# Writing the padding records in the placing stage, instead of filling whole regions during the first attention stage

## The chip, the cores and the metric

The kernel runs on one core of a Trainium2 chip. The metric is the device time of one execution in microseconds (us), as the median of several runs. The engines are TensorE (PE, with its weight loads PEld), VectorE (DVE), ScalarE (ACT), GpSimd (POOL) and SyncE (SP), which here only issues transfers (DMAs) from its own queue.

## The reference

Two transformer-like layers over 4 x 1024 tokens of 128 channels. Each of four blocks is followed by a residual addition and a layer norm:

```
x = ln(x + attention0(x))      # 8 heads, softmax
x = ln(x + ffn0(x))            # small attention, then 8 experts, top 2, gelu
x = ln(x + attention1(x))      # projections, a convolution, a scan
x = ln(x + ffn1(x))            # 8 experts, of which the last chosen one counts
```

What matters here is the last block. Its router chooses the two best of 8 experts for each token, and for expert `i` in order of number `out = where(weight_i > 0, y_i, out)`. So only the chosen expert with the higher number leaves its result, and the kernel computes one expert for each token:

```
wi = w_flat[:, i:i + 1]
h = relu(einsum('nd,hd->nh', x_flat * wi, w1[i]) + b1[i])
y = einsum('nh,dh->nd', h, w2[i]) + b2[i]
out = where(wi > 0, y, out)
```

## The kernel before

The program is a chain of stages. Each is a block in which the five engines run their own programs and meet at semaphores. A block ends with a barrier that waits for all engines. Three stages bear on the change.

`first_attention_stage` (L226) goes through 32 heads of 128 tokens, in loops of four. TensorE projects keys and queries, makes scores and mixes values; VectorE takes maxima, ScalarE exponentials, and GpSimd scales values. SyncE copies each head's keys to the other half of the partitions (`double`, L287), one head ahead. TensorE waits for this (`keys_doubled`) before a head's scores. Between these, SyncE issues one item for each head from a list: 13 loads of constants and then the filling. The filling writes blank records to `scratch`, a table in device memory in which each of the 8 experts has a region of `REGION` = 4096 + 128 rows of 136 floats. `rows_of(e)` (L294) loads the output rows of the blank records of expert `e` into the tile `blank`, and `fill(e)` (L301) writes the whole region from it in two transfers. For `e` = 8 it writes the last 8 tiles behind the regions. GpSimd clears `blank` first (L461). VectorE's first two instructions of the stage are memsets (L439, L440), for which TensorE waits.

`place_stage` (L1893) is the first part of the last block. TensorE turns the 32 tiles of 128 tokens and computes router logits, in 4 batches of 8 tiles. For each batch VectorE chooses the expert, scales the records, weighs them and computes each token's row in `scratch` (`choose`, `scale`, `weigh`, `put`). GpSimd then scatters the batch's 8 tiles to those rows, one indirect transfer of 128 rows each (L2189). After the last batch `start` holds the first free row behind each expert's records. `table` (L2145) works out from it the list of up to 40 tiles that hold records, as `tile_expert` and `tile_base`. The last tile of an expert is partly blank, and tiles behind the last one used are blank wholly; these rows go to output rows behind the end. SyncE's program is short:

```
sp.wait_ge(table_made, 1)
first = [sp.value_load(tile_base[0:1, t:t + 1], ...) for t in range(PER)]   # PER = 4
sp.wait_ge(scattered, 16 * TILES)
for t in range(PER):
    sp.dma_start(sorted_records[:, t, :], scratch[ds(first[t], TILE), :]) ...
```

`sorted_experts_stage` (L2194) loads the other 36 tiles of `scratch` by their addresses (L2252), one `value_load` and one transfer of 68 KB each, and runs each tile through its expert.

Of the kernel before, what the change touches and what calls it, by code (L numbers as in the profile page):

```python
# [7 lines left out]
F32 = mybir.dt.float32  # L8
# [4 lines left out]
ds = bass.ds  # L13


D = 128
B, S = 4, 1024
N = B * S
TILE = 128
# [6 lines left out]
E = 8  # L26


SORT_TILES = (N + E * (TILE - 1)) // TILE + 1
SORT_TILES += -SORT_TILES % 4  # L30
TABLE = SORT_TILES + 2
REGION = N + TILE
UNUSED = 8
RECORD = D + 8
DUMP = E + UNUSED
BLANK_ROWS = 8
U32 = mybir.dt.uint32
I32 = mybir.dt.int32
# [187 lines left out]
def first_attention_stage(core, xT, y, w_q, w_k, values, loads, scratch, blank_rows):  # L226

# [10 lines left out]
    with ExitStack() as st:  # L238
# [28 lines left out]
        blank = core.sb("a_blank", [D, BLANK_ROWS, RECORD], F32, st)  # L267
        blank_zero = core.sem("a_blank_zero")
        blank_rows_in = core.sem("a_blank_rows_in")
        filled = core.sem("a_filled")  # L270
# [11 lines left out]
        with nc.Block() as block:  # L282

            @block.sync
            def _(sp):
# [8 lines left out]
                def rows_of(e):  # L294

                    sp.wait_ge(blank_zero, 1)
                    if e:
                        sp.wait_ge(filled, 32 * e)
                    sp.dma_start(blank[:, :, D:].bitcast(U32), blank_rows[:, e, :, :]).then_inc(blank_rows_in, 16)

                def fill(e):  # L301

                    sp.wait_ge(blank_rows_in, 16 * (e + 1))
                    all_rows = blank[:, :, :].rearrange("p j d -> p (j d)")
                    at = e * REGION
                    if e == E:
                        at += (SORT_TILES - UNUSED) * TILE
                        sp.dma_start(scratch[at:at + UNUSED * TILE, :].rearrange("(p j) d -> p (j d)", j=BLANK_ROWS),
                                     all_rows).then_inc(filled, 16)
                        return  # L310
                    wide = [D, N // (D * BLANK_ROWS), BLANK_ROWS * RECORD]
                    sp.dma_start(scratch[at:at + N, :].rearrange("(c p j) d -> p c (j d)", p=D, j=BLANK_ROWS),
                                 all_rows.unsqueeze(1).broadcast_to(wide)).then_inc(filled, 16)
                    sp.dma_start(scratch[at + N:at + REGION, :].rearrange("(p j) d -> p (j d)", j=BLANK_ROWS),
                                 all_rows[0:TILE // BLANK_ROWS, :]).then_inc(filled, 16)

                double(0, 0)
                for head in range(TILES):
                    double(head + 1, (head + 1) % 2)
                    if head < len(loads):  # L320
                        to, at = loads[head]
                        sp.dma_start(to, at).then_inc(loaded, 16)
                    else:
                        e, at = divmod(head - len(loads), 2)
                        if e <= E:
                            if at == 0:
                                rows_of(e)
                            else:
                                fill(e)
                sp.wait_ge(filled, 16 * (2 * E + 1))  # L330
# [129 lines left out]
            def _(pool):  # L460
                nc.gpsimd.memset(blank[:, :, :], 0.0).then_inc(blank_zero, 1)  # L461
# [1425 lines left out]

PER = BANK // D

def place_stage(core, src, mean_w, ident, router, order, records, scratch, tile_expert, tile_base, loads, sorted_records,  # L1893
# [18 lines left out]
    tile_rows, rows_of_out = order[:, at:at + TABLE], order[:, at + TABLE:at + TABLE + TILES]  # L1912
    at += TABLE + TILES
    region, earlier_first = order[:, at:at + E], order[:, at + E:at + 2 * E]
    with ExitStack() as st:
# [5 lines left out]
        eps = core.sb("p_eps", [D, 1], F32, st)  # L1921
        turned = core.ps("p_turned", [TILE, 2, BANKS, BANK], st)
# [39 lines left out]
        recorded = core.sem("p_recorded")  # L1962
# [701 lines left out]
```

## Time and profile before

| | |
|---|---|
| median of 3 runs | 1737.61 us (1737.19 to 1740.08) |
| the profiled execution's own time | 1737.19 us |
| its span in the trace | 1735.3 us |
| TensorE busy | 1545.1 us, 89% |
| VectorE, ScalarE, GpSimd busy | 1321.8, 1288.9, 542.7 us |
| placing stage | about 1564.7 to 1630.4 us of the span |

The time is that of the execution on the device; the span runs from the first to the last instruction that the profiler recorded, 1.9 us shorter. Busy times count no register, semaphore or DMA-issuing instructions. All times below are counted from the start of the span.

### The profile page before, as it was taken

The page shows a single profiled execution, that of the slowest core. Times are in us where ns is not written, and L with a number is a line of the kernel's source. Part 1 is how long each engine was busy: PE and PEld are TensorE (multiplying, and loading weights), DVE is VectorE, ACT ScalarE, POOL GpSimd, SP SyncE. Part 2 cuts the span into 40 slices and gives each one's busy share as a digit, 9 for nine tenths or more (in the row PEclk, how much of TensorE's full clock was granted, in tenths as well). Part 3 has the DMA queues.
Part 4 walks back from the last instruction along what each step waited for, and adds up shares of the span by engine and source line. Part 5 has one row for each costly group of instructions (what it writes and reads, how often), then busy time and mean ns, then how long its engine had stood idle before and what let it go on. Part 6 is the DMA issues. An engine that isn't in the chain of part 4 may idle for free. (4 is left out here: it accounts for less than half of the span.)

```text
span 1735.3 us, 38769 instructions
## 1 busy us (share of the span) xinstructions
PE 1545.1 (89%) x13958; PEld 839.0 (48%) x13958; DVE 1321.8 (76%) x1885; ACT 1288.9 (74%) x2465; POOL 542.7 (31%) x757
## 2 busy tenths in 40 slices
PE   5999999999988999999999999998899965664397
PEld 4555555555553344343434444346677721223286
DVE  2777777777759999999999999954655447985475
ACT  2777777777763899989988989986688758753187
POOL 0222222222236110101011011205799805543466
PEclk8999999999995999999999999998999976886599
DMA  2121123232204010011001100005254300003220
GB/s 75 29 87 59 54 73 111 86 125 73 85 19 123 21 31 15 5 21 31 7 5 31 32 5 26 17 3 101 49 99 90 58 16 0 1 0 139 57 66 32
DMA packets 49388, 84.83 MB, mean 49 GB/s; under 512 B 19232, under 2 KB 25128, under 8 KB 48752
## 3 DMA queue, kind: packets, MB, share of 16 engines
q1 hardware_dynamic: 43888, 76.25, 16.9%
q0 software_dynamic: 5376, 6.96, 1.5%
q8 instruction: 73, 1.20, 0.3%
q14 instruction: 51, 0.42, 0.1%
HBM read 32.78 MB, written 23.92 MB: 33 GB/s over the span
## 5 line engine op out<-in xcount | busy, mean ns | idle before, releaser
L1050 ACT ACTIVATE m_probs<-m_ring 128x512 f32<-128x512 f32 x1024 | 543.1, 598 | 76.2 <-PE m_ring L966 60.4
L1129 DVE TENSOR_REDUCE m_half_max<-m_pairs 128x2 f32<-128x1024 f32 x512 | 587.9, 1215 | 11.1 <-PE m_pairs L949 10.6
L436 DVE TENSOR_REDUCE a_neg_max<-a_scores 128x1 f32<-128x1024 f32 x257 | 310.5, 1215 | 90.7 <-PE a_scores L363 90.7
L424 ACT ACTIVATE a_probs<-a_scores,a_neg_max 128x1024 f32<-128x1024 f32 x256 | 285.4, 1115 | 123.4 <-DVE a_neg_max L436 123.4
L981 PE MATMUL m_acc<-m_probs,m_v_aug 128*32 128x256 f32 (+1 forms) x4032 | 325.9, 396 | 0.0
L966 PE MATMUL m_ring<-m_q_max,m_k 32*128 32x512 f32 x1024 | 317.9, 497 | 4.0 <-DVE m_q_max L1143 2.9
L949 PE MATMUL m_pairs<-m_k,m_q 32*128 32x512 f32 x1024 | 263.4, 512 | 13.0 <-DVE m_half_max L1129 9.6
L363 PE MATMUL a_scores<-a_q,a_k_own 64*128 64x512 f32 x516 | 259.9, 620 | 6.5 <-ACT a_probs L424 5.6
L363 PE MATMUL a_scores<-a_q,a_k_other 64*128 64x512 f32 x516 | 258.3, 620 | 0.8 <-ACT a_probs L424 0.3
L966 PEld LDWEIGHTS m_ring<-m_q_max,m_k 32*128 32x128 f32 x1024 | 146.7, 183 | 216.9 <-ACT m_probs L1050 109.5
L472 POOL TENSOR_TENSOR a_scaled<-values,a_inv 128x128 f32<-128x128 f32 x256 | 102.0, 399 | 365.7 <-DVE a_inv L454 234.8
L1495 POOL TENSOR_TENSOR e_g_parts<-e_gated,e_g_parts 128x512 fp32r<-128x512 f32 x128 | 165.6, 1326 | 37.8 <-ACT e_g_parts L1420 36.4
L1454 DVE TENSOR_TENSOR e_gated<-e_up,e_gates 128x512 f32<-128x512 f32 x128 | 87.2, 690 | 86.8 <-ACT e_up L1413 78.7
L373 PE MATMUL a_mixed<-a_probs,a_scaled 128*32 128x128 f32 x4128 | 139.2, 276 | 0.0
L981 PEld LDWEIGHTS m_acc<-m_probs,m_v_aug 128*32 128x32 f32 x4032 | 79.8, 108 | 122.7 <-ACT m_probs L1050 70.6
L373 PEld LDWEIGHTS a_mixed<-a_probs,a_scaled 128*32 128x32 f32 x4128 | 104.9, 109 | 56.2 <-issue 30.3
L363 PEld LDWEIGHTS a_scores<-a_q,a_k_other 64*128 64x128 f32 x516 | 86.0, 187 | 65.4 <-issue 32.7
L949 PEld LDWEIGHTS m_pairs<-m_k,m_q 32*128 32x128 f32 x1024 | 97.3, 187 | 28.0 <-DVE m_half_max L1129 23.1
L1413 ACT ACTIVATE e_up<-e_up,e_b 128x512 f32<-128x512 f32 x128 | 84.4, 660 | 32.7 <-PE e_up L1370 32.6
L363 PEld LDWEIGHTS a_scores<-a_q,a_k_own 64*128 64x128 f32 x516 | 86.0, 187 | 33.2 <-issue 24.3
L1229 POOL CAST m_max_cols<-m_row_max 128x16 fp32r<-128x16 f32 x32 | 6.8, 212 | 281.8 <-DVE m_row_max L1135 281.1
L1420 ACT ACTIVATE e_g_parts<-e_gated 128x512 fp32r<-128x512 f32 x128 | 79.7, 624 | 7.8 <-DVE e_gated L1454 7.8
(283 smaller groups left out, 2151.7 us busy)
## 6 DMA issues: line engine op xcount, KB each, us to landing
sorted_tokens<-a_blank SPq DMA_DIRECT2D x8, 2176.0 KB
e_gates<-sorted_results SPq DMA_DIRECT2D x64, 256.0 KB, 8.5
a_k_other<-a_k_own SPq DMA_DIRECT2D x66, 128.0 KB, 2.3
m_k<-m_k_init SPq DMA_DIRECT2D x8, 512.0 KB, 6.6
m_q<-xT SPq DMA_DIRECT2D x8, 512.0 KB, 7.2
f_records<-sorted_tokens SPq DMA_DIRECT2D x40, 68.0 KB, 1.8
e_w<-e_w_dram SPq DMA_DIRECT2D x1, 2064.0 KB, 7.5
xT<-x_t_dram SPq DMA_DIRECT2D x1, 2048.0 KB, 7.8
```

Of the source, the lines that this page charges most:

```text
L363: last = nc.tensor.matmul(scores[:, slot(i), h * BANK:(h + 1) * BANK], keys[rows, p, g // 2, :], q[rows, p, :, :].rearrange("p g t -> p (g ...
L373: last = nc.tensor.matmul(mixed[32 * j:32 * j + 32, :], scaled[:, g, j, 32 * e:32 * e + 32], probs[:, g, (2 * j + e) * TILE:(2 * j + e + 1 ...
L424: nc.scalar.activation(probs[:, g, :], scores[:, slot(h * G + g), :], ACT.Exp, bias=neg_max[:, g:g + 1], accum_out=total[:, g:g + 1]).then ...
L436: nc.vector.tensor_reduce(neg_max[:, i % G:i % G + 1], scores[:, slot(i), :], AX, ALU.max, negate=True).then_inc(max_done, 1)
L472: nc.gpsimd.tensor_tensor(scaled[:, g, :, :].rearrange("p j (e c) -> p j e c", c=48)[:, :, :, 0:16], values[:, ds(b * G, G), 16 * g:16 * g ...
L949: last = nc.tensor.matmul(pairs[:, pair % 2, m, :], q[batch % 2][rows, g, at:at + TILE], k[batch % 2][rows, g, a * BANK:(a + 1) * BANK], s ...
L966: nc.tensor.matmul(o, k[batch % 2][rows, n % GROUPS, u * TILE:(u + 1) * TILE], q_max[rows, number % 2, :], start=True, stop=True).then_inc ...
L981: last = nc.tensor.matmul(acc[32 * j:32 * j + 32, of], v_aug[:, g, u, j, :], probs[:, u % SLOTS, j, of], start=(g == 0 and u == 0), stop=( ...
L1050: nc.scalar.activation(probs[:, u % SLOTS, head, :], ring[:, bank, :], ACT.Exp, scale=0.5).then_inc(ring_taken, 1)
L1129: nc.vector.tensor_reduce(half_max[:, pair // PAIRS % 2, at:at + 2], pairs[:, pair % 2, :, :], AX, ALU.max).then_inc(pair_taken, 1)
L1454: nc.vector.tensor_tensor(gated[:, n % R, :], up[:, n % R, :], gates[:, c % 2, e, :], ALU.mult).then_inc(gated_done, 1)
L1495: nc.gpsimd.tensor_tensor(g_parts[:, 1, n % R, :], gated[:, n % R, :], g_parts[:, 0, n % R, :].bitcast(F32), ALU.subtract).then_inc(lo_don ...
```

## The change

The filling and its tile, semaphores and input table are taken out of the first attention stage. The placing stage gets a tile `p_blank` with 16 blank tiles of 128 records. GpSimd clears it and copies the output rows into it from the table `order`, which is 16 columns wider. SyncE writes 8 of them to the tiles behind the regions as soon as they are set. When the last batch is placed, VectorE copies `start` into integers (`pad_at`), and SyncE reads the 8 numbers and writes one blank tile of 128 rows behind each expert's records. The first four loads of sorted records wait for these writes too.

```
 first_attention_stage:
-                def rows_of(e):
-                    sp.wait_ge(blank_zero, 1)
-                    if e:
-                        sp.wait_ge(filled, 32 * e)
-                    sp.dma_start(blank[:, :, D:].bitcast(U32), blank_rows[:, e, :, :]).then_inc(blank_rows_in, 16)
-                def fill(e):
-                    sp.wait_ge(blank_rows_in, 16 * (e + 1))
...
-                    sp.dma_start(scratch[at:at + N, :].rearrange("(c p j) d -> p c (j d)", p=D, j=BLANK_ROWS),
-                                 all_rows.unsqueeze(1).broadcast_to(wide)).then_inc(filled, 16)
-                    sp.dma_start(scratch[at + N:at + REGION, :].rearrange("(p j) d -> p (j d)", j=BLANK_ROWS),
-                                 all_rows[0:TILE // BLANK_ROWS, :]).then_inc(filled, 16)
...
-                sp.wait_ge(filled, 16 * (2 * E + 1))
...
-                nc.gpsimd.memset(blank[:, :, :], 0.0).then_inc(blank_zero, 1)
 place_stage, SyncE:
                 for to, at in loads[1:]:
                     sp.dma_start(to, at).then_inc(loaded, 16)
+                sp.wait_ge(blank_set, 1)
+                last = E * REGION + (SORT_TILES - UNUSED) * TILE
+                sp.dma_start(scratch[last:last + UNUSED * TILE, :].rearrange("(t p) d -> p t d", p=TILE),
+                             blank[:, E:, :]).then_inc(padded_done, 16)
+                sp.wait_ge(pads_known, 1)
+                for e in range(E):
+                    at = sp.value_load(pad_at[0:1, e:e + 1], min_val=0, max_val=E * REGION)
+                    sp.dma_start(scratch[ds(at, TILE), :], blank[:, e, :]).then_inc(padded_done, 16)
                 sp.wait_ge(table_made, 1)
                 first = [sp.value_load(tile_base[0:1, t:t + 1], ...
+                sp.wait_ge(padded_done, 16 * (E + 1))
                 sp.wait_ge(scattered, 16 * TILES)
 VectorE, table():
+                    then(nc.vector.tensor_copy(pad_at[0:1, :], start[0:1, :]))
+                    dve.sem_inc(pads_known, 1)
                     tt(count[:, :], start[:, :], region, ALU.subtract)
 GpSimd:
+                nc.gpsimd.memset(blank[:, :, :], 0.0).then_inc(blank_zero, 1)
+                pool.wait_ge(blank_zero, 1)
+                pool.wait_ge(order_in, 16)
+                nc.gpsimd.tensor_copy(blank[:, :, D + 1].bitcast(U32), rows_of_out[:, TILES:]).then_inc(blank_set, 1)
                 for b in range(B):
                     pool.wait_ge(copied, BANKS * (b + 1))
```

## Rows read from the trace of the kernel before

**Rows 1.** The page, engines: busy us (share of the span), instructions.

```profile
PE 1545.1 (89%) x13958; PEld 839.0 (48%) x13958; DVE 1321.8 (76%) x1885; ACT 1288.9 (74%) x2465; POOL 542.7 (31%) x757
```

**Rows 2.** Timeline of SyncE, first attention stage: start, us, queue, line, operation.

```profile
155.80 1.10 SPq L291 DMA_DIRECT2D a_k_other<-a_k_own  x2
...
212.46 1.10 SPq L291 DMA_DIRECT2D a_k_other<-a_k_own  x2
...
241.38 0.59 SPq L312 DMA_DIRECT2D sorted_tokens<-a_blank  x1
...
269.12 1.10 SPq L291 DMA_DIRECT2D a_k_other<-a_k_own  x2
```

**Rows 3.** Windows: length, busy by engine (instructions), clock, DMA share, GB/s.

```profile
184.00:198.00 14.00, 14.00 (x180) 8.04 (x178) 10.63 (x19) 10.48 (x19) 3.19 (x8) 1.00 0.18 56
...
240.00:254.00 14.00, 14.00 (x186) 7.94 (x178) 10.52 (x17) 10.48 (x20) 3.19 (x8) 1.00 0.51 183
...
1580.00:1590.00 10.00, 5.40 (x23) 4.84 (x22) 8.46 (x40) 4.06 (x21) 7.31 (x8) 0.67 0.14 50
```

**Rows 4.** DMA issues by tile: times, KB each, median us to landing.

```profile
sorted_tokens<-a_blank SPq DMA_DIRECT2D x8, 2176.0 KB
...
sorted_tokens<-a_blank SPq DMA_DIRECT2D x8, 68.0 KB
```

**Rows 5.** Timeline, start of the first attention stage (idle before, releaser).

```profile
22.71 1.00 POOL L461 MEMSET a_blank<- 128x1088 f32 x1 [22.25 <-POOLq L202]
23.43 2.62 DVE L439 MEMSET a_scaled<- 128x3072 f32 x1 [8.90 <-PEq L202]
26.42 1.76 DVE L440 MEMSET a_probs<- 128x2048 f32 x1 [0.38 <-issue]
```

**Rows 6.** Timeline of GpSimd, placing stage.

```profile
1580.55 1.08 POOL L2189 DMA_INDIRECT sorted_tokens<-p_records,p_slots  x1 [20.19 <-DVE p_slots L2141]
...
1599.62 0.95 POOL L2189 DMA_INDIRECT sorted_tokens<-p_records,p_slots  x1 [0.30 <-issue]
1605.71 0.95 POOL L2189 DMA_INDIRECT sorted_tokens<-p_records,p_slots  x1 [5.14 <-DVE p_slots L2141]
...
1625.03 0.96 POOL L2189 DMA_INDIRECT sorted_tokens<-p_records,p_slots  x1 [0.30 <-issue]
```

**Rows 7.** Timeline of VectorE, placing stage.

```profile
1564.73 0.29 DVE L2166 TENSOR_TENSOR p_turn_w<-consts_sb 128x128 f32<-128x128 f32 x1 [0.32 <-PEq L1659]
...
1599.74 0.20 DVE L2113 RECIPROCAL p_inv<-p_total 128x8 f32<-128x8 f32 x1 [3.34 <-remote]
...
1613.42 0.16 DVE L2143 COPY p_start<-p_upto 128x8 f32<-128x8 f32 x1
...
1618.15 0.19 DVE L2069 TENSOR_TENSOR tile_base<-p_base,e_order 1x42 int32<-1x42 f32 x1
```

**Rows 8.** Timelines of SyncE, loads of sorted records; last, from 1650 on.

```profile
1627.50 2.30 SPq L1993 DMA_DIRECT2D f_records<-sorted_tokens  x4
...
1631.15 20.11 SPq L2252 DMA_DIRECT2D f_records<-sorted_tokens  x19
...
1649.93 21.24 SPq L2252 DMA_DIRECT2D f_records<-sorted_tokens  x19
```

**Rows 9.** SyncE's lines L1989, L1993 (ns min/median/max, first and last start), landings.

```profile
L1989 SPq TENSOR_LOAD <-tile_base x4: 264/376/566, 1618.4 to 1620.4; - x4
...
L1989 SPq SEQ_ASSERT  x4: 11/28/374, 1619.2 to 1620.9; - x4
...
L1993 SPq FUSED_REGOPS  x4: 37/42/48, 1627.3 to 1629.3; - x4
...
DMA to landing us min/median/max: 1.7/1.8/2.1
```

**Rows 10.** Timeline of SyncE, a burst of 256 KB loads.

```profile
1190.96 10.87 SPq L1357 DMA_DIRECT2D e_gates<-sorted_results  x8
```

More of the change, by code:

```diff
@@ L26 @@
 E = 8
[L29 to L38, printed above, removed]
 class Core:
@@ L223, in _, with first_attention_stage @@
                                          ACT.Copy).then_inc(copied, 1)
-def first_attention_stage(core, xT, y, w_q, w_k, values, loads, scratch, blank_rows):
+def first_attention_stage(core, xT, y, w_q, w_k, values, loads):
     nc = core.nc
@@ L266, in first_attention_stage @@
         loaded = core.sem("a_loaded")
[L267 to L270, printed above, removed]
         CREDIT = G
@@ L292, in double @@
                                      k_own[64 * h:64 * h + 64, p, :, :]).then_inc(keys_doubled, 16)
-                def rows_of(e):
-                    sp.wait_ge(blank_zero, 1)
-                    if e:
-                        sp.wait_ge(filled, 32 * e)
-                    sp.dma_start(blank[:, :, D:].bitcast(U32), blank_rows[:, e, :, :]).then_inc(blank_rows_in, 16)
-                def fill(e):
-                    sp.wait_ge(blank_rows_in, 16 * (e + 1))
[L304 to L311, printed above, removed]
-                    sp.dma_start(scratch[at:at + N, :].rearrange("(c p j) d -> p c (j d)", p=D, j=BLANK_ROWS),
-                                 all_rows.unsqueeze(1).broadcast_to(wide)).then_inc(filled, 16)
-                    sp.dma_start(scratch[at + N:at + REGION, :].rearrange("(p j) d -> p (j d)", j=BLANK_ROWS),
-                                 all_rows[0:TILE // BLANK_ROWS, :]).then_inc(filled, 16)
                 double(0, 0)
@@ L322, in _ @@
                         sp.dma_start(to, at).then_inc(loaded, 16)
[L323 to L329, printed above, removed]
-                sp.wait_ge(filled, 16 * (2 * E + 1))
                 sp.wait_ge(keys_doubled, DUP * (TILES + 1))
@@ L1885, in _ @@
                         gate(b)
+SORT_TILES = (N + E * (TILE - 1)) // TILE + 1
+SORT_TILES += -SORT_TILES % 4
+TABLE = SORT_TILES + 2
 PER = BANK // D
+REGION = N + TILE
+UNUSED = 8
+RECORD = D + 8
+DUMP = E + UNUSED
+U32 = mybir.dt.uint32
+I32 = mybir.dt.int32
 def place_stage(core, src, mean_w, ident, router, order, records, scratch, tile_expert, tile_base, loads, sorted_records,
@@ L1911, in place_stage @@
     at = D + E * (PER_BATCH + 1)
-    tile_rows, rows_of_out = order[:, at:at + TABLE], order[:, at + TABLE:at + TABLE + TILES]
-    at += TABLE + TILES
+    tile_rows, rows_of_out = order[:, at:at + TABLE], order[:, at + TABLE:at + TABLE + TILES + DUMP]
+    at += TABLE + TILES + DUMP
     region, earlier_first = order[:, at:at + E], order[:, at + E:at + 2 * E]
@@ L1921, in place_stage @@
         eps = core.sb("p_eps", [D, 1], F32, st)
+        blank = core.sb("p_blank", [TILE, DUMP, RECORD], F32, st)
+        pad_at = core.sb("p_pad_at", [1, E], I32, st)
         turned = core.ps("p_turned", [TILE, 2, BANKS, BANK], st)
@@ L1962, in place_stage @@
         recorded = core.sem("p_recorded")
+        blank_zero = core.sem("p_blank_zero")
+        blank_set = core.sem("p_blank_set")
+        pads_known = core.sem("p_pads_known")
         table_made = core.sem("p_table_made")
+        padded_done = core.sem("p_padded_done")
         scattered = core.sem("p_scattered")
@@ L2172, in _ @@
                 dve.wait_ge(order_in, 16)
-                nc.vector.tensor_copy(records[:, :, D + 1].bitcast(U32), rows_of_out).then_inc(recorded, 1)
+                nc.vector.tensor_copy(records[:, :, D + 1].bitcast(U32), rows_of_out[:, 0:TILES]).then_inc(recorded, 1)
                 then(nc.vector.tensor_copy(counts[:, :, 0], region))
@@ L2491, in build @@
                     constants.append((tiles.q[0][:, g, :].bitcast(F32), xT[:, PAD + N:PAD + N + S]))
-                first_attention_stage(core, xT, y, w_q, w_k, values, constants, scratch, a["blank_rows"])
+                first_attention_stage(core, xT, y, w_q, w_k, values, constants)
             tiles.add(core, st)
@@ L2607, in layouts @@
         np.broadcast_to(np.arange(TABLE) * TILE, (D, TABLE)),
-        row[:, None] + TILE * np.arange(TILES),
+        row[:, None] + TILE * np.arange(TILES + DUMP),
         np.broadcast_to(np.arange(E) * REGION, (D, E)),
         np.broadcast_to(np.arange(E, 0, -1) / 16, (D, E))], axis=1).astype(np.float32)
-    behind_end = N + (row[:, None] * BLANK_ROWS + np.arange(BLANK_ROWS))
-    blank_rows = np.zeros((D, E + 1, BLANK_ROWS, RECORD - D), np.uint32)
-    for e in range(E):
-        blank_rows[:, e, :, 1] = N + TILE * e + (behind_end - N) % TILE
-    blank_rows[:, E, :, 1] = behind_end + TILE * E
     def of_channels(v):
```

1 line of the change is left out of this document (removed).

## The prediction

> **What bounds the kernel now.** I read the page first: TensorE is busy for 89% of the span, so a transfer that lies beside its work costs nothing unless it makes TensorE or its feeders wait [rows 1]. The change touches two stages, and I read each by its own view. In the first attention stage I took SyncE's own timeline, to see where the 26 transfers that go away stand between those that TensorE waits for [rows 2], and the windows of two equal stretches, one with a filling transfer and one without [rows 3]. In the placing stage I took GpSimd's timeline. There one sees 16 scatters back to back, a wait of 5.14 us for the slots of the third batch, and 16 more back to back up to 1625.99 [rows 6]. After that SyncE issues the first four loads of sorted records at 1627.50, and the next stage begins behind them [rows 8]. So the end of the placing stage is set by GpSimd's last 16 scatters and before them by the slots that VectorE makes. SyncE idles until both are done, and whatever it does before 1627.3, when its wait for the scatters ends [rows 9], is free.
>
> **Part 1, the filling leaves the first attention stage.** It issues 8 transfers of 2176 KB and 8 of 68 KB [rows 4], and by their shapes one of 544 KB and 9 loads of 32 KB, some 19 MB. They stand in the queue that also carries the doubling of the keys, which each head needs. If they delayed it, heads with a fill would be longer. Four heads without a fill run from 155.80 to 212.46, 56.66 us. The next four hold two fills and run from 212.46 to 269.12, again 56.66 us [rows 2]. TensorE is busy for 14.00 of 14.00 us in both kinds of stretch, although the DMA share goes from 0.18 to 0.51 [rows 3]. So removing 19 MB is worth 0.0 us. The cover is the head's own work: the doubling is one head ahead, and a fill of 2.2 MB at 183 GB/s takes about 12 us of a head's 14.
>
> **Part 2, one GpSimd memset leaves the start of that stage.** GpSimd clears the blank tile from 22.71 to 23.71. VectorE's first memset, for which and for the second TensorE waits (`zeroed`), begins at 23.43, 0.72 us behind GpSimd's start [rows 5]. Either this is the memset's doing or it is the slow start of a stage. For the slow start speaks that the second memset also begins 0.38 us behind the first one's end, when GpSimd has long been done. Bounds of the gain: 0 and 0.72 us. I take what is left of the 0.72 when a gap like the second one is taken off, 0.3 us.
>
> The Trainium skill, "SBUF — State Buffer", section "Who interferes with whom", says that VectorE contends with GpSimd only in the modes that use both ports, or with two SBUF inputs against a GpSimd instruction that reads SBUF. By that rule a memset beside a memset costs nothing here, unless memset is such a mode; this term would be 0, and so would the next one. The trace neither refutes nor shows it, as the 0.72 us has two readings.
>
> **Part 3, GpSimd prepares the blank tiles in the placing stage.** The memset is twice as wide (2176 against 1088 elements a partition), so 2 x 1.00 = 2.0 us [rows 5], then a small cast that waits for the order table. That ends near 1567.5; GpSimd's first scatter is at 1580.55 and it sat idle for 20.19 us before it [rows 6]. This is hidden with 13 us to spare. But the memset now lies beside VectorE's first instruction at 1564.73 [rows 7], on which TensorE's turning of the tiles and then the whole stage wait. Same rows, same bounds: 0 to +0.7 us; I take +0.3, the same reading as in part 2. If part 2 is nothing, so is this; the two go together and cancel.
>
> **Part 4, the transfer of the eight unused tiles (544 KB).** SyncE issues it behind the expert weights. From 1580 on the DMA engines are at 0.14 of their time [rows 3], so the weights are in by then; at 183 GB/s 544 KB is 3 us more. It is awaited only at the end, 40 us later. Cost 0.
>
> **Part 5, the eight padding tiles behind each expert's records.** VectorE gets one more copy after the last batch's base rows (`start`, 1613.42 to 1613.58 [rows 7]). The copy takes the place of the next instruction and ends at about 1613.8; everything in `table` moves 0.2 us later, `tile_base` from 1618.34 to 1618.54. SyncE learns of it about 0.1 us later, at 1613.9. For each expert it then reads an address and issues a transfer of 68 KB. The nearest rows are the loads of sorted records, with the same steps, the same bytes and the other direction. 19 of them span 20.11 us, (20.11 - 0.33) / 18 = 1.10 us each. While GpSimd scatters they span 21.24 us, 1.16 us each [rows 8]. As GpSimd scatters here all the time, 8 x 1.16 = 9.3, so the last is issued at 1623.2. Behind it in SyncE's program stand the four address loads that were free before: from 1618.4 to 1620.4 plus the last one's own 0.9, 2.9 us [rows 9]. They end at 1626.1. The last padding tile lands 1.7 to 2.1 us after its issue by the landings of the same size [rows 9], at the latest at 1625.3, so the new wait on it is over first. SyncE arrives at the wait for the scatters at 1626.1, 1.2 us before they let it through at 1627.3. Cost 0, and with the slack of 1.2 us gone, 1 us for each us. Queued behind this wait are only the four first loads, and with them the end of the stage.
>
> Could the padding make the scatters themselves late? A padding tile is 68 KB, 0.4 us at 183 GB/s [rows 3]; the last is issued nearly 3 us before the last scatter's descriptors are ready, so 0 to +0.4 us, and I take 0. The Trainium skill, "DMA: Bandwidth & Descriptors", section "Issuing engines are not separate DMA queues", says that transfers of SyncE and GpSimd run on the same 16 DMA engines and interleave. By that rule the upper bound would be the truth only if they meet, and the sum would be 0.4 us more.
>
> **Sum.** Profiled execution: 1737.19 us (span 1735.3 and 1.9 around it), 0.4 below the median of 1737.61. 1737.19 + 0 (part 1) - 0.3 (part 2) + 0.3 (part 3) + 0 (part 4) + 0 (part 5) = 1737.2; set against the median, **1737.6 us**. No change.
>
> **The rivals.** Within 0.2%, 3.5 us, is about what a measurement of this kernel can't tell from no change.
>
> Rival A, SyncE comes too late (slower). The place is part 5. If a padding tile costs more than 1.16 + 1.2/8 = 1.31 us, the stage ends late; from 1.16 + 4.7/8 = 1.75 us on it is over 0.2%. For it: issues of this queue can be slow, as eight in a burst took 10.87 us, 1.36 each, against 0.33 [rows 10]. With 0.77 for the address (1.10 - 0.33) that is 2.1 us a tile, 17 us for eight; SyncE is through at 1613.9 + 17 + 2.9 = 1633.8, 6.5 us late: 1744.1 us. Against it: those were bursts of 256 KB with no address load between them, and the 68 KB loads beside GpSimd's scatters kept 1.16. Chance 0.13.
>
> Rival B, VectorE's stall goes away (faster). In the third batch VectorE waits 3.34 us before a reciprocal for nothing that the program holds back [rows 7], and shorter ones lie around it; the fourth batch runs the same code without. They are why GpSimd waits 5.14 us. If they hang on how the program lies in memory or on what transfers run, the change may move them. GpSimd's next scatter could then start at 1599.62 + 0.95 + 0.3 = 1600.87 and not at 1605.71: -4.8 us, 1732.8 us. Against it: VectorE's program is the same up to that place. Chance 0.12. The opposite, such a stall falling into the table behind the last batch, would make `tile_base` come up to 8 us late and cost about (1618.5 + 8 + 2.9) - 1627.3 = 2 us or somewhat more: 1740 to 1743. Chance of its being over 0.2%: 0.05.
>
> Rival C, the filling did cost something: if only the queue's end or the memory were freed, the gain would be part 2's upper bound with part 3 at 0, -0.7 us, 1736.9. This lies within "no change" and can't be told from it by the time, only by the profile.
>
> **How the numbers follow.** My forecast with rival C in it 0.70, A 0.13, B 0.12, the stall in the table 0.05. Faster 0.12, within 0.2% 0.70, slower 0.18. The likeliest case's own range is 1735.5 to 1740.5: the bounds of parts 2, 3 and 5 and the 2.9 us that the runs before spread over. To hold 8 in 10 the range reaches down to rival B and a part of the way to A: 1732.8 to 1742.0.
>
> **What the profile after would show.** Head period unchanged at 56.66 us for four heads, DMA share low through the stage (part 1). VectorE's first memset there 0.3 us nearer to the stage's start, or as late as before (part 2). GpSimd's memset of 2.0 us beside VectorE's first instruction of the placing stage, and whether that one starts later than 0.05 us behind SyncE's first issue (part 3). Eight issues of SyncE between about 1614 and 1623, 1.1 to 1.2 us apart, four address loads, then a wait of about 1 us that GpSimd's last scatter ends (part 5). The prediction is wrong if SyncE's four loads come later after GpSimd's last scatter than 1.5 us, or if GpSimd's wait for the third batch isn't about 5 us.

## The result, and the profile after

The changed kernel takes 1747.06 us (median of 14 runs, 1739.60 to 1757.48) where the kernel before took 1738.13 us on the same chips (14 runs, 1731.82 to 1746.36). The ratio is 1.0061, with a 95% interval of 1.0044 to 1.0078: slower by 8.9 us. Forecast were 1737.6 us and no change. Two later sets of runs, on other chips, gave 1.0063 (1.0036 to 1.0089) and 1.0043 (1.0020 to 1.0065). In the first of these two sets one execution of the kernel before took 2320 us, at a mean clock of 0.55 where the others had 0.929 or more, and one of another version likewise; the ratios leave such executions out.

The profiled execution of the changed kernel took 1751.21 us, with a span of 1749.1. It is cut most simply at the barriers between the stages. Between barriers the first attention stage lasted 470.40 us (before 470.47), the placing stage 73.00 (before 65.73) and the second attention stage 668.22 (before 662.14). Two stages grew clearly, by 7.3 us the placing stage and by 6.1 us a stage whose instructions the change doesn't touch. The others differ by up to 2.2 us either way, 0.5 us in sum. The second attention stage comes up again at the end of the experiments.

The page, engines, as in [rows 1]:

```profile
PE 1548.7 (89%) x13958; PEld 837.6 (48%) x13958; DVE 1320.5 (75%) x1886; ACT 1289.0 (74%) x2465; POOL 545.2 (31%) x758
```

**The attention stage is unchanged.** SyncE's timeline of the changed kernel, which answers [rows 2]; the lines of the code now have lower numbers:

```profile
155.78 1.10 SPq L274 DMA_DIRECT2D a_k_other<-a_k_own  x2
...
212.43 1.10 SPq L274 DMA_DIRECT2D a_k_other<-a_k_own  x2
...
226.32 43.87 SPq L274 DMA_DIRECT2D a_k_other<-a_k_own  x8
```

Four heads still take 212.43 - 155.78 = 56.65 us. The windows of [rows 3], in the changed kernel: the second stretch held a fill before and now holds none, at a DMA share of 0.09 where it was 0.51, and the engines' busy times are the same.

```profile
184.00:198.00 14.00, 14.00 (x180) 8.04 (x178) 10.62 (x19) 10.48 (x19) 3.20 (x8) 1.00 0.18 56
240.00:254.00 14.00, 14.00 (x186) 7.96 (x178) 10.52 (x17) 10.48 (x20) 3.21 (x8) 1.00 0.09 19
```

VectorE's first memset, with GpSimd's beside it gone (as in [rows 5]), begins just as late:

```profile
23.47 2.62 DVE L391 MEMSET a_scaled<- 128x3072 f32 x1 [8.82 <-PEq L190]
```

**The placing stage.** Three timelines of the changed kernel, and two lines of its code. The first is GpSimd's; its last scatter is cut from a run of equal lines, as in [rows 6]:

```profile
1570.92 1.91 POOL L2161 MEMSET p_blank<- 128x2176 f32 x1 [4.34 <-POOLq L1610]
...
1612.18 0.95 POOL L2170 DMA_INDIRECT sorted_tokens<-p_records,p_slots  x1 [5.40 <-DVE p_slots L2116]
...
1631.14 0.96 POOL L2170 DMA_INDIRECT sorted_tokens<-p_records,p_slots  x1 [0.30 <-issue]
```

VectorE's, which answers [rows 7]:

```profile
1570.96 0.29 DVE L2143 TENSOR_TENSOR p_turn_w<-consts_sb 128x128 f32<-128x128 f32 x1 [0.32 <-PEq L1610]
...
1608.11 0.20 DVE L2088 RECIPROCAL p_inv<-p_total 128x8 f32<-128x8 f32 x1 [4.05 <-issue]
...
1619.88 0.16 DVE L2118 COPY p_start<-p_upto 128x8 f32<-128x8 f32 x1
1620.07 0.16 DVE L2122 CAST p_pad_at<-p_start 1x8 int32<-1x8 f32 x1
...
1624.69 0.19 DVE L2044 TENSOR_TENSOR tile_base<-p_base,e_order 1x42 int32<-1x42 f32 x1
```

SyncE's, which answers [rows 8]:

```profile
1573.58 0.41 SPq L1956 DMA_DIRECT2D sorted_tokens<-p_blank  x1
1622.11 16.48 SPq L1961 DMA_DIRECT2D sorted_tokens<-p_blank  x8
1641.52 1.95 SPq L1968 DMA_DIRECT2D f_records<-sorted_tokens  x4
```

And the instructions of SyncE's two lines for the eight padding tiles (ns min/median/max, first and last start), to be held against [rows 9]:

```profile
L1960 SPq TENSOR_LOAD <-p_pad_at x8: 5/268/699, 1620.3 to 1637.5; - x8
L1960 SPq FUSED_REGOPS  x8: 3/152/699, 1620.8 to 1637.8; - x8
L1960 SPq SEQ_ASSERT  x8: 1/18/690, 1621.1 to 1638.0; - x8
...
L1961 SPq MOVE sorted_tokens<-p_blank x8: 2/29/697, 1621.4 to 1638.2; - x8
L1961 SPq DMA_DIRECT2D sorted_tokens<-p_blank x8: 2/332/708, 1622.1 to 1638.3; - x8
```

One sees this. SyncE begins on time, 0.1 us after `pad_at` is ready. Then eight tiles take from 1620.3 to 1638.6, 18.3 us and not 9.3. The last five lines show how: the median of each instruction is its normal duration, and the maximum is 0.69 to 0.71 us for all of them, also for a MOVE between registers, whose median is 29 ns. The minimum is as odd: an issue with a median of 332 ns is once recorded with 2 ns, a register load of 268 ns with 5. From the fifth instruction (1621.4) to 1634.8, 13.4 us, the trace has 21 steps from one instruction's start to the next: 11 of 0.7 us, 4 of 1.4 us and 6 of under 0.05 us. That is 0.64 us an instruction on average, where it is 0.18 afterwards, when a tile took 1.09 us. GpSimd's last scatter was issued by 1632.10, and SyncE's first load of records followed at 1641.52, 9.42 us later. Before it was 1.51 us (1625.99 to 1627.50, [rows 6, 8]). This distance, called D below, is what the change costs in this stage: 9.42 - 1.51 = 7.9 us. The last scatter came 0.1 us earlier in its stage, and the four loads behind D took 0.35 us less (1.95 against 2.30), which with 0.15 us at the barrier leaves the 7.3.

### The profile page after: what moved, and what is told of

It is laid out like the page before. It is cut to its first block and busy times, and to the rows that moved or that the text cites. A ratio compares the mean times of both kernels' runs of the same rounds, so it can differ in the third digit from the quotient of the medians.

```text
span 1749.1 us, 38791 instructions
## 1 busy us (share of the span) xinstructions
PE 1548.7 (89%) x13958; PEld 837.6 (48%) x13958; DVE 1320.5 (75%) x1886; ACT 1289.0 (74%) x2465; POOL 545.2 (31%) x758
## 3 DMA queue, kind: packets, MB, share of 16 engines
q1 hardware_dynamic: 32096, 58.14, 13.4%
## 5 line engine op out<-in xcount | busy, mean ns | idle before, releaser
L932 PE MATMUL m_acc<-m_probs,m_v_aug 128*32 128x256 f32 (+1 forms) x4032 | 331.0, 401 | 0.0
L900 PE MATMUL m_pairs<-m_k,m_q 32*128 32x512 f32 x1024 | 263.4, 512 | 13.4 <-DVE m_half_max L1080 9.6
```

Of the source, the lines that this page charges most:

```text
L900: last = nc.tensor.matmul(pairs[:, pair % 2, m, :], q[batch % 2][rows, g, at:at + TILE], k[batch % 2][rows, g, a * BANK:(a + 1) * BANK], s ...
L932: last = nc.tensor.matmul(acc[32 * j:32 * j + 32, of], v_aug[:, g, u, j, :], probs[:, u % SLOTS, j, of], start=(g == 0 and u == 0), stop=( ...
```

## The experiments

The expectations below name these theories. Theory 1: instructions have to be fetched, and fetching is late while GpSimd's scatters run close together, 0.7 us a step, on any engine. It would explain VectorE's stall of [rows 7] too, since that lies beside the first run of scatters and has the same steps. Theory 2: code that runs for the first time is slow, whatever runs beside it. Theory 3: only SyncE's loads of registers and its issues are late beside scatters, not their fetching.

### The padding after the last scatter (pads_late)

```
                 sp.wait_ge(pads_known, 1)
+                sp.wait_ge(scattered, 16 * TILES)
                 for e in range(E):
```

> The changed kernel, but SyncE writes the eight padding tiles only when all scatters have landed, so nothing of GpSimd runs beside them. The quantity is D, from the end of GpSimd's last scatter to SyncE's first load of sorted records (1.5 us before the change, 9.4 us after it). Theory 1 (SyncE's program has to be fetched, and a fetch takes 0.7 us while scatters run): the pads go at 1.1 us each, D = 1.4 + 8 x 1.1 + 2.9 = 13.1 us. Theory 2 (code that runs for the first time is slow wherever it stands, whatever else runs): 2.06 us each, D = 1.4 + 17 + 2.9 = 21 to 22 us. Theory 3 (SyncE's register loads and issues themselves are slow beside scatters, not their fetching): 13.1 us as theory 1.

SyncE's timeline, and the register loads of the eight tiles:

```profile
1626.41 8.08 SPq L1962 DMA_DIRECT2D sorted_tokens<-p_blank  x8
1636.97 1.94 SPq L1969 DMA_DIRECT2D f_records<-sorted_tokens  x4
...
L1961 SPq TENSOR_LOAD <-p_pad_at x8: 265/270/477, 1625.1 to 1633.1; - x8
```

The eight issues span 8.08 us, so a tile costs (8.08 - 0.33) / 7 = 1.11 us, and D is 13.26 us. The number of theories 1 and 3 was 13.1, that of theory 2 was 21 to 22. The same eight tiles are cheap as soon as no scatters run beside them, and the durations of a few ns are gone too (the shortest load takes 265). Theory 2 falls. (1746.5 us, one run.)

### The padding as a loop (pads_loop)

```
-                for e in range(E):
-                    at = sp.value_load(pad_at[0:1, e:e + 1], ...)
+                with sp.Fori(0, E) as e:
+                    at = sp.value_load(pad_at[0:1, ds(e, 1)], ...)
```

> The changed kernel, with the eight padding tiles written in a hardware loop of SyncE instead of eight copies of the code; same transfers, same order. Theories 1 and 2: only the first pass is slow (about 3 to 4 us), the other seven take 1.1 to 1.5 us each, so the pads are issued by about 12 to 14 us after the start and not 16.5; the address loads behind are new code again. D = 3 to 6 us, 4 to 6 us faster than the changed kernel. Theory 3: each pass is as slow as before, D about 9.4 us and no gain.

SyncE's timeline:

```profile
1631.08 20.14 SPq L1961 DMA_DIRECT2D sorted_tokens<-p_blank  x8
1653.86 1.93 SPq L1968 DMA_DIRECT2D f_records<-sorted_tokens  x4
```

No gain: D is 12.85 us. In the loop's second pass, whose instructions had run already, the branch and the MOVE took 0.7 us each as well. So the expectation of theory 1 failed: repeating the same code doesn't help, as it should if lateness came of code that isn't at hand. Theory 3 failed too, for the late ones are of every kind. That D is even 3.4 us longer than with straight code is the loop's own: SyncE was late until 2.8 us after the last scatter's issue, as before, and had three tiles out by then; the five behind took 1.54 us each, as a pass has more instructions than a tile of the straight code, which takes 1.09. The ratio to before, 1.0109 (1.0073 to 1.0144, four runs), isn't the loop's price: in its profile the second attention stage lasted 676.57 us, 14.4 more than before, and all four runs had a mean clock of 0.933 or less.

### The padding on ScalarE, and on both (pads_act, pads_split)

In pads_act ScalarE issues all eight tiles at the end of its program, in pads_split SyncE those of even experts and ScalarE those of odd ones:

```
+                act.wait_ge(blank_set, 1)
+                act.wait_ge(pads_known, 1)
+                for e in range(E):                  # pads_split: range(1, E, 2)
+                    at = act.value_load(pad_at[0:1, e:e + 1], ...)
+                    act.dma_start(scratch[ds(at, TILE), :], blank[:, e, :]).then_inc(padded_done, 16)
```

> The changed kernel, with the eight padding tiles written by ScalarE's queue, which is idle then; SyncE only loads its four addresses and waits. Theories 1 and 2: ScalarE's code there is new too and runs beside the scatters, so it is as slow: the last pad is issued 16 us after the copy of start, D about 7 to 9 us, at most 2 us faster than the changed kernel. Rival: the slowness is SyncE's alone; then ScalarE issues at 1.1 us each, is done before the scatters, D = 1.5 us, and the kernel is 7 to 8 us faster than the changed one, level with the one before.

> The changed kernel with the padding tiles shared: SyncE writes four, ScalarE's queue the other four at the same time. Theory 1 (each queue's own code is fetched slowly beside scatters, 0.7 us a step): the two run side by side at about 2 us a tile, so the tiles are out 8 to 9 us after the copy of start, before the scatters are done, and only SyncE's four address loads are left slow behind them. D (from the end of GpSimd's last scatter to SyncE's first load of records) 2 to 4.5 us, against 9.4 in the changed kernel and 1.5 before; 5 to 7 us faster than the changed kernel, 0 to 3 slower than the one before. Rival (the slowness is a limit that both queues share, such as the bandwidth or the DMA engines): the eight take 16 us together whoever issues them, D about 7.

ScalarE's timeline of pads_act and the issues of its line L2031, and then ScalarE's and SyncE's timelines of pads_split:

```profile
1617.13 16.38 ACTq L2031 DMA_DIRECT2D sorted_tokens<-p_blank  x8
...
L2031 ACTq DMA_DIRECT2D sorted_tokens<-p_blank x8: 4/343/727, 1617.1 to 1633.2; - x8
```

```profile
1615.31 8.40 ACTq L2035 DMA_DIRECT2D sorted_tokens<-p_blank  x4
...
1615.95 12.99 SPq L1961 DMA_DIRECT2D sorted_tokens<-p_blank  x4
```

ScalarE is late as SyncE is, 16.38 us for eight issues, with the same 0.7 us steps; only its first three tiles ran at the normal pace. D is 7.11 us, the ratio 1.0044 (1.0018 to 1.0070). So it isn't a property of SyncE. Split, D is 5.25 us and the ratio 1.0031 (1.0003 to 1.0058), between the 2 to 4.5 us of theory 1 and the 7 of a limit that the engines share. The tiles themselves speak more for the second: the last was out 15 us after `start` was made, where theory 1 had 8 to 9 and the shared limit 16. SyncE's four issues alone span 12.99 us.

### All scatters late, in the kernel before (late_scatter)

```
             def _(pool):
+                pool.wait_ge(slots_done, B)
                 for b in range(B):
```

> The kernel before the change, but GpSimd begins its 32 scatters only when VectorE has made the slots of all four batches. Theory 1 (code fetched beside scatters is slow): VectorE's waits of together 8.5 us in the third batch and ScalarE's of 2.9 us vanish, since no scatter runs there; the scatters then begin about 40 us after the stage's start, and the stage is about 19 to 20 us longer. Theory 2 (new code is slow at that place of the program whatever else runs): the waits stay at the same instructions, and the stage is about 28 us longer.

VectorE had no stall: `start` was made 40.8 us into the stage, against 49.0 before. The stage took 85.60 us, 19.9 more than before (forecast 19 to 20), as all 32 scatters now stand behind the last slots. D stayed at 1.51. This shows that VectorE's lost 8 us came from the scatters beside it, and not from its program. (1764.52 us, one run.) SyncE's four address loads fell into the run of scatters, whose first was issued at 1612.17, and were not late:

```profile
L1989 SPq TENSOR_LOAD <-tile_base x4: 263/364/482, 1616.6 to 1618.7; - x4
```

So an engine's first dozen instructions can go at the normal pace as late as 7 us into a run of scatters.

### A pause between two batches of scatters, in the kernel before (pause_before, pause_before_again)

```
                 for b in range(B):
+                    if b == 1:
+                        pool.wait_ge(chosen_done, 3)
                     pool.wait_ge(copied, BANKS * (b + 1))
```

> The kernel before the change, with one more wait on GpSimd: its second batch of scatters begins only when VectorE has chosen the experts of the third batch. Theory 1: GpSimd pauses about 2 us between the first and the second batch, VectorE's program is fetched ahead in that pause, its waits of 8.5 us in the third batch shrink to under 2, and GpSimd's wait of 5.1 us before the third batch goes; the last scatter ends 2 to 3.5 us earlier, ratio about 0.998 to 1.000. Rival (the pause is too short for a fetch, or VectorE's code is fetched only when it gets there): the waits come back after the pause, the last scatter ends where it did or up to 2 us later.

> The kernel before, in which GpSimd waits ahead of its second batch of scatters until VectorE has done the gates of the third. Fetch theory: VectorE's stall is gone as in the earlier run (placing stage 63.3 us where before has 65.7), so 2.4 us off, ratio 0.9986, and with 5 more rounds an interval that may leave out 1. The rival (the 2.4 us were that profile's luck): ratio 1.000 and a placing stage of 65 to 66 us.

GpSimd's and VectorE's timelines of pause_before:

```profile
1587.98 0.96 POOL L2191 DMA_INDIRECT sorted_tokens<-p_records,p_slots  x1 [2.84 <-DVEq L2107]
...
1600.19 0.16 DVE L2143 COPY p_start<-p_upto 128x8 f32<-128x8 f32 x1
```

GpSimd waits 2.84 us once; the wait of 5.14 us for the third batch [rows 6] is gone, because VectorE no longer stalls. The stage takes 63.31 us, 2.4 less (64.52 in the second set). The ratios are 0.9987 (0.9966 to 1.0008) and 0.9966 (0.9946 to 0.9985), on two chips. It is the one version here that is faster than both kernels, clear of the noise in the second set alone. The stage accounts for 1.2 to 2.4 us of it; that the second set shows more (medians 3.3 us apart, a ratio worth 5.9 us) stays unexplained. SyncE, too, was late in it: its four address loads (L1989), 2.9 us before [rows 9], now began at 1605.0 beside the scatters and ended at 1614.7, with medians of 0.46 and 0.70 us. They stayed hidden. Two of that line's instructions:

```profile
L1989 SPq TENSOR_LOAD <-tile_base x4: 5/464/700, 1605.0 to 1611.9; - x4
L1989 SPq SEQ_ASSERT  x4: 37/699/710, 1605.8 to 1614.0; - x4
```

### The same pause in the changed kernel (pause_after)

> The changed kernel with the same wait of GpSimd ahead of its second batch of scatters. Fetch theory: VectorE makes the start indices at +41 us of the stage and not at +49, SyncE's eight padding tiles begin there, still at some 2 us each beside the scatters, and end at +57 to +59, before or with the last scatter; from the last scatter's issue to the load of records 1.5 to 3.5 us, not 9.4; stage 63.5 to 66 us, ratio 0.998 to 1.001. Rival (the padding costs SyncE or the queues its 7 us wherever it is put): stage 68 to 71 us, ratio 1.002 or more.

VectorE's and then SyncE's timeline:

```profile
1608.13 0.16 DVE L2118 COPY p_start<-p_upto 128x8 f32<-128x8 f32 x1
...
1610.87 23.36 SPq L1961 DMA_DIRECT2D sorted_tokens<-p_blank  x8
1637.16 1.95 SPq L1968 DMA_DIRECT2D f_records<-sorted_tokens  x4
```

This one went against my theory. `start` was made 8 us earlier, as forecast, and SyncE began at once. But its eight issues took 23.36 us and not some 16, D was 11.25 us, the stage took 72.38 and the ratio was 1.0038 (1.0013 to 1.0062). The rival had a ratio of 1.002 or more and a stage of 68 to 71 us, so the stage was longer than either forecast. Of 19 steps 10 were now 1.4 us, 9 were 0.7 us and none was near nothing, 1.07 us an instruction, and they went on to 3.9 us behind the last scatter's issue. So lateness is no fixed price of an instruction. SyncE got four tiles out while it was late, in 21 us here and in 14.5 us in the changed kernel, and did the rest at the normal pace behind them.

### Forty readings of a constant (probe_before)

In the kernel before, with no transfer started and no result waited for:

```
+                sp.wait_ge(order_in, 16)
+                sp.wait_ge(recorded, 3)
+                for _ in range(40):
+                    sp.value_load(order[0:1, 0:1].bitcast(I32), min_val=0, max_val=1)
                 sp.wait_ge(table_made, 1)
```

> The kernel before, in which SyncE, from the moment that the first batch of records is ready (+15.9 us of the placing stage), reads the same constant 40 times into registers, three instructions to a reading, 0.5 us when undisturbed, no transfer started by any. Theory 1 (an engine whose next instructions are not at hand gets each 0.7 or 1.4 us late while GpSimd's scatters run close together): the readings begin at 0.5 us each, turn to 2 to 4 us each within the first run of scatters (+16 to +29), are fast again from about 3 us after that run ends to the start of the next (the lull of 5 us), and slow again in the second run until 3 to 4 us after the last scatter; the 40 readings take over 35 us, where they would take 20. Rival (only instructions around a load from memory or a started transfer are late, or only those that wait for VectorE's results): 0.5 us each throughout, 20 us in all.

The readings' line (L1991), in four windows: 1579.1 to 1585.4, 1585.4 to 1604.3, 1604.3 to 1613.9 and 1613.9 to 1623.

```profile
L1991 SPq TENSOR_LOAD <-e_order x10: 264/270/483, 1579.2 to 1584.9; - x10
...
L1991 SPq TENSOR_LOAD <-e_order x7: 14/700/1407, 1585.5 to 1602.2; - x7
...
L1991 SPq TENSOR_LOAD <-e_order x18: 13/267/271, 1604.4 to 1613.6; - x18
...
L1991 SPq TENSOR_LOAD <-e_order x5: 2/688/701, 1614.0 to 1619.3; - x5
```

GpSimd's timeline of the same run, the first scatters of its two runs:

```profile
1581.56 1.08 POOL L2193 DMA_INDIRECT sorted_tokens<-p_records,p_slots  x1 [20.19 <-DVE p_slots L2145]
...
1600.68 0.96 POOL L2193 DMA_INDIRECT sorted_tokens<-p_records,p_slots  x1 [0.31 <-issue]
1609.38 0.96 POOL L2193 DMA_INDIRECT sorted_tokens<-p_records,p_slots  x1 [7.74 <-DVE p_slots L2145]
```

Ten readings in 6.3 us, then seven in 18.9 us, then eighteen in 9.6 us, then five in 7.5 us: fast, late, fast, late. The first late stretch begins 4 us after the first scatter and ends 2.7 us after the last one of the run (1601.64 to 1604.36); the second begins 4.6 us after the next run's first. All forty took 42.2 us, where forty at the pace of the eighteen, 0.53 us, would take 21. The rival of an even 0.5 us falls.

VectorE was later beside the readings, though its program is the same and waits for none of them. GpSimd's wait for the third batch is 7.74 us here; in the eleven other profiles that have this wait it lies between 5.14 and 5.82. The stage took 68.41 us, 2.7 more than before. With the eight tiles of pads_split this speaks for something that the engines share, and not for a delay that each has by itself. It is one run.

The queues of this kernel in the first late stretch, 1586 to 1604 (packets, MB, share of 16 engines), and then those of the changed kernel from 1620 to 1636:

```profile
q0 software_dynamic: 425, 0.91, 14.8%
q14 instruction: 1, 0.01, 0.2%
```

```profile
q0 software_dynamic: 352, 0.77, 14.3%
q1 hardware_dynamic: 666, 0.33, 6.9%
```

The profile has queues of its own for instructions. In the changed kernel none of their packets falls between 1620 and 1636, where SyncE was late for 13 us. So "instructions have to be fetched" isn't shown, and this speaks against fetching through those queues. Bytes and rows alone don't do it either: SyncE's loads of sorted records move tiles of the same 128 rows and 68 KB every 1.10 us, with no scatters in a row beside them, and nothing is late [rows 8].

### What of it is the fills (fills_and_pads three times, after_again, after_third)

fills_and_pads is the kernel before, fills kept, with everything that the change adds to the placing stage. It differs from the changed kernel in the fills alone. after_again and after_third are the changed kernel.

> The kernel before with its filling kept in the first attention stage, and the changed kernel's padding added in the placing stage (both write blank records). If the whole cost is the padding's: first attention stage 470.4 us as in both kernels, placing stage 73 us as in the changed one, ratio as for the changed kernel, 1.004 to 1.008. Rival: taking the filling away has a price or a gain of its own elsewhere; then this kernel's time stands between the two or outside them by more than 3 us.

> The changed kernel once more, beside a kernel that keeps the fills. The placing stage is 7.3 us longer than in the kernel before whatever the chip does, so a ratio of 1.0042 is the least. Theory F (with the fills gone from the attention stage, TensorE's granted clock falls earlier in the second attention stage, which costs some 6 us in a part of the executions): the ratio is again above 1.005, the granted clock is at or below 0.935 in a third or more of the executions, and in the kernel with the fills in hardly any. Theory H (the earlier fall of the clock comes with the chip and the hour, whatever the kernel): ratio 1.003 to 1.005, and as many low clocks here as in the kernel with the fills.

> The kernel before with the padding tiles and all that the change adds to the placing stage, and with the fills kept: it differs from the changed kernel in the fills alone. Placing stage 71 to 73 us (5.4 to 7.3 over before). Theory F: ratio 1.002 to 1.004, and the changed kernel is 2 us or more slower than this one. Theory H: the two agree within 2 us.

> The changed kernel a third time, beside the kernel that keeps the fills. Theory F (without the fills the clock falls earlier more often): 2 us or more above that kernel's median, and more executions at a granted clock of 0.935 or less. Theory H (no effect of the fills): the medians within 2 us of one another, ratio to before 1.004 to 1.006.

> The kernel with the fills and the padding tiles a third time. Placing stage 71 to 73.5 us, so 5.5 to 7.8 us over before: ratio 1.003 to 1.0045 by either theory; by theory F the changed kernel of this call is 2 us or more above it, by theory H within 2 us.

| | ratio to before | 95% | placing stage, us |
|---|---|---|---|
| fills_and_pads | 1.0021 | 1.0002 to 1.0041 | 71.16 |
| after_again | 1.0063 | 1.0036 to 1.0089 | 73.35 |
| fills_and_pads_again | 1.0048 | 1.0025 to 1.0071 | 73.01 |
| after_third | 1.0043 | 1.0020 to 1.0065 | 73.53 |
| fills_and_pads_third | 1.0038 | 1.0014 to 1.0063 | 72.02 |

The kernel with the fills kept has 5.4, 6.3 and 7.3 us of extra placing stage, the changed kernel 7.3, 7.6 and 7.8. So most of the cost comes without removing anything; the rest, 1.2 us on average, may be chance or the fills, and three profiles each don't tell. The first ratio, 1.0021, lay below the 1.004 to 1.008 that were forecast. The changed kernel lies 2.3 and 0.9 us above the other in the two sets on a common chip, once above and once below the line of 2 us that the expectations drew, within what the intervals leave open. The profiles say more. The stage that was 6.1 us longer in the changed kernel's first profile is the second attention stage. Windows (length, busy by engine, granted clock, DMA share, GB/s) of the changed kernel and of after_again:

```profile
1080.00:1160.00 80.00, 79.44 (x782) 32.61 (x782) 63.45 (x63) 72.16 (x138) 11.75 (x17) 0.98 0.04 10
...
1080.00:1160.00 80.00, 79.43 (x796) 32.98 (x792) 63.61 (x63) 73.02 (x141) 11.74 (x17) 1.00 0.04 10
```

And the 17 us from 1157 on, in the kernel before, after_again, the changed kernel, fills_and_pads_third and late_scatter (which keeps the fills as well):

```profile
1157.00:1174.00 17.00, 13.26 (x136) 5.90 (x134) 7.79 (x20) 12.72 (x25) 3.39 (x5) 1.00 0.06 11
...
1157.00:1174.00 17.00, 13.47 (x137) 6.00 (x136) 7.86 (x21) 12.71 (x26) 3.38 (x5) 1.00 0.06 11
...
1157.00:1174.00 17.00, 17.00 (x113) 5.38 (x116) 8.08 (x20) 10.44 (x20) 1.27 (x1) 0.50 0.00 1
...
1157.00:1174.00 17.00, 17.00 (x110) 5.39 (x114) 8.52 (x22) 10.99 (x22) 1.27 (x1) 0.52 0.00 1
...
1157.00:1174.00 17.00, 17.00 (x110) 5.23 (x112) 8.28 (x21) 10.73 (x21) 1.27 (x1) 0.51 0.00 1
```

In every one of these profiles TensorE's granted clock goes from 2.4 to 1.2 GHz before the stage ends. In the first two it does so at about 1174 us, 8 us before the end (in the kernel before it is 1.00 up to 1174 and 0.51 from there to 1182). In the other three it does so at about 1157, 17 us earlier, after TensorE was busy for all of the 7 us before, as in the first two, and this stage is then 6 us longer (668.2 against 662.1). The changed kernel had it in its first profile and not in after_again (span 1742.9 us); fills_and_pads_third (span 1748.8) and late_scatter had it with the fills in place. So it isn't the removal of the fills that brings it about. Whether the removal makes it more frequent stays open: a mean clock of at most 0.934 had 9 of 22 executions of the changed kernel and 8 of 24 with the fills kept in the two sets on a common chip, which can't be told apart. In the first runs, on different chips, it was 17 of 38 and 1 of 10.

## Why the prediction was wrong

**Parts 1 and 4** held. Four heads take 56.65 us without fills, where 56.66 was forecast, and the 544 KB transfer, issued at 1573.58, met nothing. Rival C, that the fills did cost something, falls by the same rows.

**Parts 2 and 3**: the bounds held, my choice within them didn't. VectorE's first memset in the attention stage begins at 23.47 without GpSimd's beside it, against 23.43, and in the placing stage its first instruction begins 0.05 us behind SyncE's with GpSimd's memset beside it (1570.96 and 1570.91). Both terms are 0 and not -0.3 and +0.3, so the sum was untouched. The rule of the Trainium skill, "SBUF — State Buffer", section "Who interferes with whom", by which an instruction of VectorE with no or one SBUF input is not held up outside the modes that use both ports, and one with two inputs not by an instruction of GpSimd that only writes, agrees with both rows: the first is a memset, the second a TENSOR_TENSOR beside GpSimd's memset.

**Part 5 is the step that failed**: "As GpSimd scatters here all the time, 8 x 1.16 = 9.3". The eight tiles took 18.3 us, 2.3 each. The 1.16 came from loads in the next stage, beside scatters that stand apart; I took "while GpSimd scatters" as one condition. There the scatters stand 1.8 to 2.6 us apart, in the placing stage 1.26 us. That the distance makes the difference is argued from these two stages; no run varied it alone. The rest of the part was right. SyncE began 0.1 us behind `pad_at`, the four address loads took 2.9 us behind the last tile (1638.6 to 1641.5), and with the slack of 1.2 us gone each us cost one: 18.3 - 9.3 - 1.2 = 7.8, against 7.9 measured in D. The warning stood in my own rows: of the address loads in [rows 9] one SEQ_ASSERT took 374 ns with a median of 28, and a reciprocal of VectorE waited 3.34 us for nothing [rows 7]. I listed the second as rival B, tied to the program's place in memory, and didn't ask what else ran beside it.

The possible 0.4 us by which the padding might delay the scatters wasn't seen: the last scatter's issue ended 61.25 us into the stage, before 61.37.

**Rival A** had the size (6.5 us late, 1744.1 us) but not the cause. It made the issue dear; the issue's median stayed at 332 ns, and instructions of every kind around it were late. The cause is shown this far: beside scatters in close order SyncE, ScalarE and VectorE advance in steps of 0.7 or 1.4 us (the changed kernel, pads_act, probe_before), SyncE at 0.64 us an instruction instead of 0.18 in the changed kernel, and at their normal pace without them (SyncE in pads_late, VectorE in late_scatter). **Rival B**'s stall is of the same kind. It didn't go away with the change (4.05 us before the reciprocal now), but does when the scatters leave VectorE a pause (pause_before).

**What stays open.** What makes an instruction late isn't settled. Fetching is argued against by the loop and by the empty instruction queues. The executions timed here, of either kernel, carry a span and clock from the profiler. The Trainium skill, "NOTIFIC — the notification-queue block", section "Overflow: three behaviours, one of which stalls the engine", says that this block's internal pipeline holds engines back rather than lose a record. No run here shows whether it did. Two things that were measured would fit a hold-up in the recording: the late stretches hold instructions recorded with 2 to 15 ns whose undisturbed duration is 265 ns and more, so the recorded times can't be those of the work alone, and VectorE was later beside SyncE's readings. Neither shows it. If that were the cause, part of the 7 us would belong to the recording; that, too, stays open, and a run without the recording would be a test. And of the 8.9 us, 7.3 are the placing stage. The other 1.6 us aren't shown; they may come with executions in which the clock fell early, more of which the changed kernel may have had by chance.

## What to carry to other kernels

A price per instruction holds only beside the same neighbours: before taking "1.16 us a tile" from another stage, look at how densely GpSimd's scatters stand there, and look at the minima and maxima of an instruction line, not only at its median. Work that is put on an idle queue during back-to-back scatters isn't free; here eight small transfers of 1.1 us each took 18.3 us and moved the end of the stage. 19 MB of fills beside a busy TensorE cost nothing, so there was nothing to win by removing them, and the pause of a few us between scatters, which costs GpSimd 2.84 us and saves its wait of 5.14, was the only version that gained, by 1.2 to 2.4 us in the stage.

## What the hardware showed that I had not expected

- Beside scatters of 128 rows issued every 1.26 us, instructions of SyncE, ScalarE and VectorE come in steps of 0.7 or 1.4 us, register instructions included, with some recorded almost at once in between (6 of 21 steps of SyncE in the changed kernel). In probe_before this began 4.0 and 4.6 us after a run's first scatter and ended 2.7 us after the issue of its last; with 24 scatters in a row (pause_after) half of the steps were 1.4 us and they ended 3.9 us after it.
- An engine may run on for a while: ScalarE did three tiles at the normal pace from 1616.2 on, in the midst of scatters, where SyncE did four to six instructions in the changed kernel, pads_loop, pause_before and pause_after, and all twelve instructions of its four address loads in late_scatter.
- A loop is late for as long as straight code is (to 2.8 us after the last scatter's issue, against 2.7).
- Forty readings of a constant by SyncE came with 2 us more of VectorE's stall (7.74 us in GpSimd's wait against 5.14 to 5.82).
